# Score products of a grouped attention, made per query head on halves of the tensor array's columns

## The reference, cut to what matters

```python
def _gqa(q, k, v):
    scale = 1.0 / np.sqrt(q.shape[-1])
    scores = jnp.einsum('bsghd,btgd->bghst', q, k) * scale
    p = jax.nn.softmax(scores, axis=-1)
    return jnp.einsum('bghst,btgd->bsghd', p, v)
```

## Time and profile before

| | |
|---|---|
| three runs | 633.56, 634.34, 635.05 us; median 634.34 us |
| profiled execution, first to last instruction | 632.0 us |
| PE busy | 576.7 us, 91% |
| PEld busy | 468.2 us, 74% |
| DVE busy | 494.6 us, 78% |
| ACT busy | 369.1 us, 58% |
| POOL busy | 365.9 us, 58% |
| score products (L2258) | from 168.9 to 481.5 us of the span |

### The profile page before, as it was taken

How to read it: one execution, slowest core, us unless ns; L and a number is a source line. 1 busy time by engine, 2 the same in 40 slices (tenths; PEclk the granted TensorE clock), 3 DMA queues, 4 the chain that set the end, 5 groups by cost and what they waited for, 6 DMA issues and landing times.

```text
span 632.0 us, 10614 instructions
## 1 busy us (share of the span) xinstructions
PE 576.7 (91%) x3735; PEld 468.2 (74%) x3738; DVE 494.6 (78%) x924; ACT 369.1 (58%) x669; POOL 365.9 (58%) x299
## 2 busy tenths in 40 slices
PE   3999679959869999999988999999999999999996
PEld 1664225635548888988977889888889888888886
DVE  4697999775999998999998889999997956333333
ACT  1559657757766776776766676667665235434221
POOL 4101495014578787868659967676777634855431
PEclk9999999988989999999998999999999999999999
DMA  7892113015512131031192141222210100310001
GB/s 219 272 348 77 60 50 117 34 67 152 180 33 106 35 111 58 1 134 35 48 357 96 37 124 57 86 84 85 59 43 18 35 0 3 117 37 30 1 2 67
DMA packets 44564, 54.87 MB, mean 87 GB/s; under 512 B 8416, under 2 KB 30816, under 8 KB 44512
## 3 DMA queue, kind: packets, MB, share of 16 engines
q1 hardware_dynamic: 44512, 54.20, 26.5%
HBM read 41.60 MB, written 12.58 MB: 86 GB/s over the span
## 4 chain that ended last, share of the span: by engine, by line
PE 64%; DVE 6%; POOL 3%; issue 3%; ACT 2%; DVEq 0%; POOLq 0%; ACTq 0%
PE g_proj L2217 13%; PE g_proj L2303 8%; PE g_scores L2258 7%; PE g_turn L2247 6%; PE g_op L2284 5%; PE g_op L474 3%; PE g_op L475 2%; PE g_op L476 2%; PE g_proj L459 2%; PE g_proj L461 2%; PE g_proj L460 2%; PE g_turn L2267 2%; PE g_op L2225 1%; POOL g_rs L1615 1%; PE g_turn L459 1%
## 5 line engine op out<-in xcount | busy, mean ns | idle before, releaser
L1615 POOL TENSOR_TENSOR g_rs<-g_ve,neg_half 128x4 f32<-128x4 f32 x80 | 83.7, 1052 | 36.4 <-DVE g_ve L1727 36.0
L1636 POOL TENSOR_TENSOR g_cat<-g_yb,g_kb 128x1024 fp32r<-128x1024 bf16 x32 | 70.9, 2224 | 41.3 <-DVE g_yb L1782 41.3
L2217 PE MATMUL g_proj<-w_hi,g_xqc 128*128 128x512 f32 x192 | 84.4, 439 | 6.7 <-ACT g_qn L2005 4.1
L2217 PE MATMUL g_proj<-w_lo,g_xqc 128*128 128x512 f32 x192 | 76.2, 397 | 0.0
L503 POOL TENSOR_TENSOR m_h_lo<-m_h,m_h_hi 128x512 fp32r<-128x512 f32 x32 | 41.4, 1297 | 57.1 <-ACT m_h_hi L490 57.1
L1727 DVE TENSOR_REDUCE g_ve<-g_sq 128x4 f32<-128x516 f32 x80 | 54.8, 685 | 16.9 <-ACT g_sq L1979 14.9
L2258 PEld LDWEIGHTS g_scores<-g_qkT 128*128 128x128 f32 x512 | 60.9, 192 | 2.7 <-issue 1.4
L2258 PE MATMUL g_scores<-g_qkT 128*128 128x64 f32 x512 | 61.0, 272 | 0.0
L2247 PE MATMUL g_turn<-ident,g_qn 128*128 128x128 f32 x384 | 58.2, 278 | 1.8 <-DVE g_qn L1740 1.5
L1979 ACT ACTIVATE g_sq<-g_proj 128x512 f32<-128x512 f32 x80 | 47.8, 597 | 16.7 <-PE g_proj L2217 15.2
L2247 PEld LDWEIGHTS g_turn<-ident,g_qn 128*128 128x128 f32 x384 | 44.8, 143 | 11.7 <-DVE g_qn L1740 3.6
(11 more groups left out here) (242 smaller groups left out, 1662.2 us busy)
## 6 DMA issues: line engine op xcount, KB each, us to landing
kvx_rows<-f_kept SPq DMA_DIRECT2D x24, 256.0 KB, 2.4
g_ksq<-kvx_rows SPq DMA_DIRECT2D x8, 512.0 KB, 4.5
g_kraw<-kvx_rows SPq DMA_DIRECT2D x16, 256.0 KB, 3.2
g_v<-kvx_rows SPq DMA_DIRECT2D x8, 512.0 KB, 4.2
m_raw<-in_L_W SPq DMA_DIRECT2D x16, 256.0 KB, 3.0
c_raw<-in_L_wqT SPq DMA_DIRECT2D x4, 512.0 KB, 6.2
f_w_ctx<-in_L_wkvxT SPq DMA_DIRECT2D x4, 512.0 KB, 8.0
c_praw<-in_L_wprojT SPq DMA_DIRECT2D x4, 512.0 KB, 5.6
```

The source lines that it names most:

```text
L1615: G.tensor_tensor(rs[:, at % NORMS, :], ve[:, at % NORMS, :], k["half"][:, 0:4], ALU.pow).then_inc(q["rs_done"], 1)
L1636: G.tensor_tensor(cat[:, h].rearrange("p h (b s) -> p b h s", b=2), yb[:, h, :].rearrange("p (b h s) -> p b h s", b=2, s=SEQ), kb[:, h, :] ...
L2217: last = T.matmul(bank(n, i)[:], xqc[:, n % 2, view * KT + c_, :], w[:, c_, :], start=c_ == 0 and part == 0, stop=c_ == KT - 1 and part == 1)
```

## The change

In `scores`, each product is split in two: head 0's 64 columns of the stationary operand and head 1's are loaded and multiplied by themselves, and their outcomes go to partitions 0 to 63 and 64 to 127 of the same bank. The built program gives the first the position (0, 0) and the second the position (0, 64) in the array, each 128 rows by 64 columns. What is computed, and where it lies, stays the same; 8 products per half become 16, and 16 pairs of instructions become 32.

```diff
                         for b in range(2):
                             rows = slice(b * SEQ, (b + 1) * SEQ)
-                            last = T.matmul(sp_[:, (g * 2 + b) * SEQ:(g * 2 + b + 1) * SEQ], qkT[:, n % 2, 2 * kv + b, :],
-                                            qkT[:, n % 2, HEADS + kv, rows], start=True, stop=True)
+                            for half in range(2):
+                                at = slice(half * SEQ, (half + 1) * SEQ)
+                                last = T.matmul(sp_[at, (g * 2 + b) * SEQ:(g * 2 + b + 1) * SEQ], qkT[:, n % 2, 2 * kv + b, at],
+                                                qkT[:, n % 2, HEADS + kv, rows], start=True, stop=True)
                     last.then_inc(q["sc_done"], 1)
```

## The result

The changed kernel takes 627.36 us (median of 4 runs, 626.91 to 629.34) against 634.15 us before (median of 4, 633.56 to 635.05): a ratio of 0.9893 with a 95% interval of 0.9866 to 0.9921. It is faster by about 1%, clear of the noise; 627.2 us were forecast. A second set of runs on another occasion had a median of 629.20 us, a ratio of 0.9909 (0.9891 to 0.9927).

A forecast was written before the change was run, and what follows sets the result against it. TensorE, busy 91%, looked like the bound, but gains depended on who is late at `turn_p(n, 0)`. Tile gains 1.5 + 1.3 + 3.4 + 0.9 = 7.1 us took 634.3 to 627.2 us; own range 625 to 631, with rival 3 624.5 to 637.5.

The forecast's parts named there:

- The block: One score block on TensorE: from 1.73 to 1.30 us, as in attend, the halves loading and multiplying side by side.
- s: Saving per score block on TensorE: 0.43 us taken, 0.86 per tile; bounds from 0.87 to -2.16.
- The best end of the bounds: Score block with no cost of entering or leaving the halves: 0.87 us, s = 0.87, whole time 626.2 us.
- Rival 1: Score block: halves load one after the other, each half as long; s = -0.43, 645.5 us; chance 0.16.
- Rival 2: Score block: load and product of both halves strictly in turn; block 3.89, some 695 us; chance 0.05.
- Tiles 0 and 7: TensorE stands still 4.1 and 3.2 us after their score blocks; shorter blocks lengthen the waits, gain 0.
- Tiles 1, 3, 5: GpSimd, busy through x_raw until normalise, holds turn_p(n, 0); gain 0, TensorE's wait grows from 0.30 to 1.16.
- Tiles 2, 4, 6: Room of 0.98 at turn_p, but VectorE waits only 0.52 in the tile; gain 0.5 each, 1.5 us.
- Tile 8: In half 1 GpSimd is busy with the low halves and normalise(8, 1), which turn_p(8, 1) follows; gain 0.
- Tiles 9, 10: Room of 0.67 between normalise(9, 0) and turn_p; gain 0.66 each, 1.3 us.
- Tiles 11 to 14: Room of 1.0 at turn_p, and VectorE's waits of 1.07 give way; gain 0.86 each, 3.4 us.
- Tile 15: Second score block is on the chain, with the experts' products behind it on TensorE; gain 0.86, say 0.9 us.

The follow-up runs named there:

- the gap experiment: GpSimd's centring of x_raw (tiles 1, 3, 5) moved ahead of the third g_rs: from the changed kernel 625.54 us, from the kernel before 633.79 us.
- The shorter `g_cat`: The changed kernel with the centring in GpSimd's gap and half of each second g_cat left out in tiles 1 to 6: 622.60 us, ratio 0.9821.
- the one try at it: The changed kernel with VectorE's maximum and subtraction of the next tile's first scores put between the two liftings: 629.84 us, ratio 0.9928.

## Why the prediction was right, step by step

- **The block.** Right in kind: the loads set the pace, products run beside them, the halves go side by side. The term was a little mis-sized: 1.30 was forecast from `attend`, 1.22 it is with the cost of entering and leaving, s = 0.51 in place of 0.43. Of the 0.43 that was read out of `attend` for entering and leaving, 0.35 came (1.22 - 0.87): 0.09 ahead of the block, 0.05 behind it, the rest inside. The best end of the bounds (a block of 0.87) was not reached.
- **Rival 1** put the halves one after another. That does happen, if the products are ordered so, and then costs 5.5 us; in the order of the change it does not. Its argument that TensorE might not issue faster than one instruction per 34 ns falls: four start every 58 ns.
- **Rival 2** falls with it. The Trainium skill, page "TensorE: Matmul & The Clock Gate", section on packing small matmuls, lets a load overlap with running products only where the row groups differ. Here both halves have all 128 rows, and 1024 loads and products take 36.9 us. Moreover, halving the columns of the load with the product's 64 moving columns unchanged took the pace of a pair from 0.108 to 0.058, so the product adds next to nothing and runs beside a load. The measurement decides. The estimate from the same section's 2.38 for three strips was a factor of 1.59 for two. From start to next start it is 1.73 / 1.08 = 1.60, with the later entry 1.73 / 1.17 = 1.48, with the cost of leaving 1.73 / 1.22 = 1.42.
- **Tiles 0 and 7**: nothing gained there, as forecast; the long waits grew.
- **Tiles 1, 3, 5**: nothing gained, as forecast, and for the reason given; the gap experiment shows it. The wait grew to 0.99 and not 1.16: of the two blocks' 1.02, 0.34 was already lost at the bank, which the prediction did not have, and 0.30 + 1.02 - 0.34 = 0.98.
- **Tiles 2, 4, 6**: 0.27 each, not 0.5. This step failed: "TensorE could come 0.98 earlier, and with 0.86 it does", limited by VectorE's 0.52. It looked for room at `turn_p` only and overlooked two places earlier on TensorE's own way. The second block cannot start before VectorE frees the bank: in tile 4 it starts at 262.39 after, 262.40 before, and stands idle for 0.34 ahead of it. And the projection behind the output waits for GpSimd's row, which takes another 0.4. So of 2 x 0.51 = 1.02 a tile, 0.27 is left. The shorter `g_cat` gave the row's 0.4 back. What the bank's 0.34 is worth by itself is not shown, since the one try at it lengthened a lifting; by the rows of tile 4 the projection would still have had to wait for GpSimd's row until 267.68.
- **Tile 8**: nothing between its second `turn_p` and that of tile 6, as forecast.
- **Tiles 9, 10**: 0.82 and 0.63, forecast 0.66 each; `turn_p(n, 0)` waits 0.08 for GpSimd in both, where 0.2 was forecast.
- **Tiles 11 to 14**: 1.04, 1.04, 0.93 and 1.00, forecast 0.86 each with room for 1.0. That is s itself, 2 x 0.51 = 1.02: nearly the whole saving passes, as forecast, and only s was too small. The room of the earlier trace rows just suffices, as tile 11 after shows: `normalise(11, 0)` ends at 405.09, and TensorE comes at 405.17 without having waited.

```profile
404.04 1.05 POOL L1625 TENSOR_TENSOR g_ex<-g_ex,g_rc 128x512 f32<-128x512 f32 x1
...
405.17 0.66 PE L2269 MATMUL g_turn<-ident,g_ex 128*128 128x128 f32 x4
```

- **Tile 15**: 0.73 at `turn_p`, of which 0.3 is lost behind it; forecast 0.9. The experts' products were taken to be held by TensorE alone, but one of them waits for GpSimd's `m_h_lo` and keeps 0.34.

So the stretches give 6.7 us where 7.1 were forecast, with errors that offset each other: 0.7 us too much in the even own tiles and 0.5 in tile 15, against about 0.6 too little in tiles 11 to 14 and 0.1 in tiles 9 and 10. That 627.36 lies within 0.2 of 627.2 is in part luck: the second set's median lies 2.0 above. That half of the 13.8 us would come out was forecast; by the measured s, 6.7 of 32 x 0.51 = 16.3 do, some 0.4.

## What to carry to other kernels

Small products that fill half of the array's columns (here f32, 128 x 64 by 64 columns) can run two abreast, if neighbours in the program use different halves; in blocks of one half and then the other, the same products lose it all. What a shorter block is worth is found tile by tile, at the place where the engines meet, and there at the engine that now comes last: 0.82 us became 2.88 by moving one GpSimd instruction of 1.90 us into a gap. A wait that vanishes is no gain by itself; look half a tile further on for where it went.

## What was not expected of the hardware

- A second column half costs next to nothing: 544 instructions of one half take 36.5 us, 1024 of both 36.9.
- VectorE's lifting in bf16 took 1.53 us where it started beside GpSimd's running `g_cat`, and 0.69 by itself, in tile 11 for one. No experiment was made on this alone. The Trainium skill, page "SBUF — State Buffer", section "Who interferes with whom", has a VectorE instruction with two inputs in SBUF and a GpSimd instruction that reads SBUF block each other, the later one until the earlier is done. The 1.53 agree with it: the `g_cat` it started beside ends at 261.44 + 2.15 = 263.59, and the lifting 0.55 after that.
- The same kernel's executions differ at the long wait of tile 7: from the second `turn_p` of tile 6 to that of tile 8 the changed kernel takes 42.74 us in one profile and 43.34 in the other. Granted clock there, from 320 to 350 us (us, PE busy, PEclk, DMA share, GB/s), in the changed kernel's two profiles:

```profile
320.00:350.00 30.00, 24.06 (x239) 0.94 0.57 186
```

```profile
320.00:350.00 30.00, 24.14 (x234) 0.89 0.58 196
```

In both profiles TensorE stood still for 3.8 to 3.9 us. In the first the clock falls from its upper to its lower level (1.00 to 0.50) 1.4 us after the wait has ended, in the second some 2 us before it ends; the lower level lasts some 3.6 us (0.06 x 30 / 0.5) in the first and some 6.6 in the second. The kernel before with the centring in the gap shows 0.89 too, so it is not of the change. Together with the start, which moved by up to 2.4 us between the profiles, it is why small parts were read from stretches of the profile and not from whole times.
